# A graph layer's per-edge filters made by TensorE alone, one TensorE increment a turn, and gathers that wait for VectorE's message

## The chip, the cores and the metric

One NeuronCore of a Trainium2 chip runs the kernel. It has a matrix engine (TensorE, PE in the profile), a vector engine (VectorE, DVE), an activation engine (ScalarE, ACT), GpSimd (POOL), which here writes the descriptors of the gathers, and SyncE (SP), which starts plain transfers. The engines are ordered by semaphores: an instruction increments one when it ends, another waits until it has a value. The metric is the device time of one run in microseconds (us); lower is better.

## The reference

The kernel computes one message-passing layer on a graph with 6,250 nodes and 206,250 edges that are sorted by their target, with 128 features:

```python
h = jnp.maximum(_layernorm(x, axis=-1), 0.0)
W = silu(dist_feat @ fw1 + fb1) @ fw2 + fb2      # 206250 x 128, from 50 numbers an edge
x2 = silu(h @ aw1 + ab1) @ aw2 + ab2             # 6250 x 128, the node table
msg = W * x2[src]
agg = jax.ops.segment_sum(msg, dst, num_segments=h.shape[0])
out = silu(agg @ ow1 + ob1) @ ow2 + ob2
return x + h + out
```

## The kernel before

**Start.** The nodes lie in 49 tiles of 128, handled in 7 chunks. VectorE takes statistics (L557), ScalarE normalizes (L413), TensorE transposes and multiplies (L813, L819, L824), VectorE adds a bias (L571), and SyncE writes the rows to a node table in device memory (L321). Meanwhile GpSimd gathers 48 tiles of raw x rows (L369) for six "early" pairs; it waits ahead of some of them for a chunk of the table (`table_at`). When the whole table is written, GpSimd starts on the table gathers (L381).

**Turns.** The edges lie in 202 pairs of two groups of 4 tiles, 1,024 edges in a pair. A Python loop, `turns`, gives each engine its code for pair 0, 1, 2, ...; each engine's order is fixed when the program is written, and there is no scheduler. For pair s:

- TensorE `hidden` (L876): first filter layer into PSUM tile `hid_ps`, of which there is one. It increments `hid_sum`.
- ScalarE `silu_hid` (L444): SiLU from `hid_ps` into `hid[s % 2]`; increments `hid_done`.
- TensorE `filters` (L884): second filter layer, back into `hid_ps`, with features in the rows; increments `across`.
- ScalarE `add_fb2` (L450): adds the bias column, `hid_ps` into `hid[s % 2]`; increments `biased`.
- TensorE `by_edge` (L891): 8 transposes into `fil_ps[s % 2]`, edges in the rows; increments `fil_done`. It waits for `red_done` of pair s - 2, whose messages lay in that tile.
- VectorE `message` (L665) multiplies by the gathered rows in `xg[i % 3]` and increments `msg_done`; then a row sum (L668), a mask (L672) and a second row sum (L668), which increments `red_done`. Two one-hot tiles are built (L655, L657).
- TensorE `add_up` (L899): sums of pair s - 2 by matmuls with the one-hot tiles.

The next pair's `hidden` is issued before this pair's `by_edge`, and its `filters` after. Between the pairs stand steps of node tasks (`task`), which use a PSUM tile of their own.

**Gathers.** One pair's gathers are 8 indirect transfers of 128 rows, 8 instructions of GpSimd, into one of `XG` = 3 buffers. The early pairs have none, so that 195 pairs with 8 gathers and one with 4 make 1,564 in all. Ahead of pair s GpSimd has one wait: `pool.wait_ge(fil_done, run(s - REACH))` with `REACH` = 1. Since `by_edge` of s - 1 waited for `red_done` of s - 3, this says also that the buffer is free. `run(c)` only adds a fixed offset to a count.

## Time and profile before

| what | value |
|---|---|
| time, median of 3 runs | 2037.55 us (2035.7 to 2040.6) |
| span of the profiled execution, first to last instruction | 2356.9 us |
| time of the profiled execution outside its span | not given by the profile |
| GpSimd (POOL) busy in it | 1526.1 us, 65% |
| TensorE (PE) busy, weight loads (PEld) beside it | 1290.8 us and 700.7 us |
| VectorE (DVE), ScalarE (ACT) busy | 1191.7 us and 520.7 us |
| TensorE's granted clock, mean | 0.74 of full |

The profile is one execution, recorded by the hardware profiler. The rows below are of three kinds. A group of instructions reads: line, engine, operation, output<-inputs, shapes, count | busy us in all, mean ns of one | idle us of the engine just before them, and what ended it. A row of the timeline reads: start, us taken, engine, line, operation, and in brackets how long the engine had been idle and what ended that. "issue" is idle time for which the profile shows no waited-for instruction; "remote" is a wait whose releaser the profile could not name.

### The profile page before, as it was taken

To read this page: it belongs to the slowest core of one execution; us is meant where nothing else is said; L and a number is where in the kernel's file an instruction comes from. 1 tells how busy PE (TensorE), PEld (TensorE's weight loads), DVE (VectorE), ACT (ScalarE), POOL (GpSimd) and SP (SyncE) were. 2 spreads that over 40 slices of the span, in tenths; PEclk is the share of its full clock that TensorE was granted. 3 is DMA by queue.
4 is the path that set the end of the run, shared out by engine and by line. 5 is a ranking of instruction groups with operands and counts; after the bars stand their busy time and mean duration, and the time that the engine had idled before them with its cause. 6 is when DMAs were issued, how large, how long until landed. Compare 5 with 4: busy or idle time off the path is not lost.

```text
span 2356.9 us, 13198 instructions
## 1 busy us (share of the span) xinstructions
PE 1290.8 (55%) x4526; PEld 700.7 (30%) x4526; DVE 1191.7 (51%) x1497; ACT 520.7 (22%) x545; POOL 1526.1 (65%) x1619
## 2 busy tenths in 40 slices
PE   3454555655565557555655565555564566554645
PEld 2222333332232323223322232222232233322323
DVE  4455445555455445544544564445444454444545
ACT  3322222222121122122212221222121122121211
POOL 5556666667666666666666666666666676666665
PEclk9686777777786768776877786777686777677867
DMA  4421222212221212212212221222221222212211
GB/s 148 144 76 45 82 58 71 79 51 85 82 83 45 83 50 81 87 46 81 86 51 78 80 85 50 80 65 65 82 85 48 82 54 81 85 45 82 59 46 44
DMA packets 62293, 171.47 MB, mean 73 GB/s; under 512 B 27088, under 2 KB 29648, under 8 KB 59024
## 3 DMA queue, kind: packets, MB, share of 16 engines
q0 software_dynamic: 51584, 105.75, 16.8%
q1 hardware_dynamic: 8192, 61.32, 6.9%
q10 hardware_dynamic: 2448, 3.54, 0.4%
q8 instruction: 36, 0.59, 0.1%
q14 instruction: 33, 0.27, 0.0%
HBM read 164.08 MB, written 6.42 MB: 72 GB/s over the span
## 4 chain that ended last, share of the span: by engine, by line
another core or an unknown queue 30%; POOL 24%; PE 18%; issue 16%; ACT 9%; DVE 2%; DMA 0%; SPq 0%; POOLq 0%; ACTq 0%; DVEq 0%
POOL xg L381 24%; PE banks L884 9%; PE banks L876 4%; ACT hid L444 4%; ACT hid L450 4%; PE banks L891 2%; PE banks L824 1%; PE banks L899 1%; ACT hs L469 0%; DVE stats L557 0%; PE banks L819 0%; DMA xs<-in_x 0%; PE banks L944 0%; DVE sums L668 0%
## 5 line engine op out<-in xcount | busy, mean ns | idle before, releaser
L381 POOL DMA_INDIRECT xg<-node_table,src x1564 | 1479.0, 946 | 777.6 <-issue 451.3
L884 PE MATMUL banks<-hid,wts 128*128 128x512 f32 x806 | 534.4, 798 | 556.3 <-ACT hid L444 437.9
L665 DVE TENSOR_TENSOR banks<-banks,xg 128x1024 f32<-128x1024 f32 (+1 forms) x198 | 241.4, 1219 | 1070.2 <-DMA xg<-node_table,src 607.2
L668 DVE TENSOR_REDUCE sums<-banks 128x128 f32<-128x1024 f32 (+1 forms) x408 | 494.0, 1211 | 13.7
L876 PE MATMUL banks<-attr,wts 50*128 50x512 f32 x806 | 284.4, 786 | 383.1 <-ACT hid L450 206.4
L444 ACT ACTIVATE hid<-banks,cols 128x1024 f32<-128x1024 f32 x202 | 224.7, 1112 | 887.9 <-remote 672.4
L450 ACT ACTIVATE hid<-banks,cols 128x1024 f32<-128x1024 f32 x202 | 224.6, 1112 | 865.6 <-remote 376.6
L884 PEld LDWEIGHTS banks<-hid,wts 128*128 128x128 f32 x806 | 180.6, 249 | 746.6 <-ACT hid L444 465.7
L891 PE MATMUL banks<-ident,hid 128*128 128x128 f32 x1612 | 283.5, 333 | 40.1 <-issue 38.1
L891 PEld LDWEIGHTS banks<-ident,hid 128*128 128x128 f32 x1612 | 224.6, 170 | 237.1 <-issue 228.6
L672 DVE TENSOR_TENSOR banks<-banks,other 128x1024 f32<-128x1024 f32 (+1 forms) x204 | 248.7, 1219 | 7.0
L876 PEld LDWEIGHTS banks<-attr,wts 50*128 50x128 f32 x806 | 73.5, 220 | 446.0 <-issue 238.9
L899 PEld LDWEIGHTS banks<-onehot,sums 128*128 128x128 f32 x816 | 146.0, 227 | 126.9 <-issue 119.7
L899 PE MATMUL banks<-onehot,sums 128*128 128x88 f32 x816 | 134.1, 297 | 6.2 <-DVE sums L668 6.2
L369 POOL DMA_INDIRECT e_x<-in_x,e_src x48 | 45.8, 955 | 38.1 <-DVE res L571 22.6
L657 DVE SCALAR_TENSOR_TENSOR onehot<-iota,ends,onehot 128x88 f32<-128x88 f32 x202 | 62.5, 310 | 10.0 <-remote 2.9
L655 DVE TENSOR_SCALAR onehot<-iota,ends 128x88 f32<-128x88 f32 x202 | 55.2, 273 | 0.1
L824 PE MATMUL banks<-node_wts,mid 128*128 128x128 f32 x194 | 31.8, 323 | 21.8 <-ACT mid L420 11.6
L824 PEld LDWEIGHTS banks<-node_wts,mid 128*128 128x128 f32 x194 | 29.1, 231 | 25.6 <-ACT mid L420 23.6
L813 PE MATMUL banks<-ident,hs 128*128 128x128 f32 x97 | 16.0, 304 | 18.4 <-issue 18.4
L831 PE MATMUL banks<-wts,mid 128*128 128x128 f32 x98 | 23.9, 385 | 0.6 <-ACT mid L478 0.6
L819 PE MATMUL banks<-hT,node_wts 128*128 128x512 f32 (+2 forms) x28 | 16.2, 716 | 11.7 <-remote 11.7
(83 smaller groups left out, 282.9 us busy)
## 6 DMA issues: line engine op xcount, KB each, us to landing
attr<-in_attr SPq DMA_DIRECT2D x25, 2048.0 KB
xg<-node_table,src POOLq DMA_INDIRECT x1564
out<-res ACTq DMA_DIRECT2D x8, 256.0 KB
xs<-in_x SPq DMA_DIRECT2D x3, 512.0 KB, 6.6
node_table<-res SPq DMA_DIRECT2D x3, 512.0 KB
out<-res ACTq DMA_DIRECT2D x5, 192.0 KB
spare<-in_dst SPq DMA_DIRECT2D x1, 808.0 KB
src<-in_src SPq DMA_DIRECT2D x1, 808.0 KB
```

Source lines behind the costliest of these rows:

```text
L381: pool.indirect_dma_start(xg[:, i % XG, j, :], None, table[:, :], bass.IndirectOffsetOnAxis(ap=src[:, s * L + j:s * L + j + 1], axis=0))\
L444: act.activation(hid[:, s % 2, 0:n], hid_ps[:, 0:n], ACT.Silu, bias=cols[:, 0:1]).then_inc(hid_done, 1)
L450: act.activation(hid[:, s % 2, 0:n], hid_ps[:, 0:n], ACT.Identity, bias=cols[:, 3:4]).then_inc(biased, 1)
L657: dve.scalar_tensor_tensor(out=to[:, 1, :], in0=nodes, scalar=ends[:, 1, s:s + 1], in1=to[:, 0, :], op0=ALU.is_equal, op1=ALU.subtract).th ...
L665: dve.tensor_tensor(to, to, rows_of, ALU.mult).then_inc(signal, 1)
L668: return dve.reduce_sum(sums[:, at, m, :], of.rearrange("p j f -> p f j"), AX.X)
L672: dve.tensor_tensor(to, to, other[:, t:t + n].rearrange("p (j o) -> p j o", o=1).to_broadcast([P, n, F]), ALU.mult).then_inc(signal, 1)
L824: i = pe.matmul(to[:, j * P:(j + 1) * P], mid[:, j * P:(j + 1) * P], weights, start=True, stop=True)
L876: i = pe.matmul(hid_ps[:, GC * half:GC * half + GC], fw1_s[at, :], attr[at, cols_of], start=True, stop=True)
L884: i = pe.matmul(hid_ps[:, at], w["fw2_s"][:, :], hid[:, s % 2, at], start=True, stop=True)
L891: i = pe.transpose(fil_ps[s % 2][:, at], hid[:, s % 2, at], ident[:, :])
L899: i = pe.matmul(sum_ps[:, to:to + WIN], sums[:, at, m, :], onehot[:, s % OH_SETS, m, :], start=False, stop=stop and m == 1)
```

## The change

It has seven parts.

1. `filters` takes the SiLU output as the stationary operand, 8 matmuls of 128 columns, and so puts edges in the rows by itself. The bias comes first into the same PSUM tile, by two bf16 matmuls of 512 columns of `ones_b` with `fb2_rows`. `by_edge` and `add_fb2` are gone, and `across`, `biased` with them.
2. `hidden` runs two pairs ahead (`FILL` = 2) and follows `filters`.
3. TensorE increments one semaphore a turn, `pe_turn`, with the last matmul of `hidden(s + 2)`. Whoever waited for `hid_sum`, `fil_done`, `n_tr`, `n_l1` or `n_l2` now waits for a count of `pe_turn`.
4. VectorE's message of pair s waits for `pe_turn` at `after(s)`, which is `hidden(s + 2)`.
5. GpSimd waits, ahead of pair number i with gathers, for the message of pair number i - 3.
6. The 8 VectorE operations that split the bias into three bf16 rows (`fb2_part`, `fb2_rest`, `fb2_rows`), which ran only on a rarely used branch at the end, now stand on VectorE ahead of the first statistics, behind a wait for the `rows` transfer.
7. ScalarE's first turn applies SiLU to pairs 0 to 2, later turns to s + 2.

```diff
-REACH = XG - LAG
+FILL = 2
...
+def after(s):
+
+    return run(s + FILL)
...
-                    pool.wait_ge(fil_done, run(s - REACH))
+                    pool.wait_ge(msg_done, run(MAIN_TURNS[i - XG]))
...
             def silu_hid(s):
                 n = tiles_in(s) * P
-                act.wait_ge(hid_sum, run(s))
+                act.wait_ge(pe_turn, run(s))
                 act.activation(hid[:, s % 2, 0:n], hid_ps[:, 0:n], ACT.Silu, bias=cols[:, 0:1]).then_inc(hid_done, 1)
...
-            def add_fb2(s):
-                n = tiles_in(s) * P
-                act.wait_ge(across, run(s))
-                act.activation(hid[:, s % 2, 0:n], hid_ps[:, 0:n], ACT.Identity, bias=cols[:, 3:4]).then_inc(biased, 1)
-
             def pair(s):
-                for a in ((0, 1) if s == 0 else (s + 1,)):
+                for a in range(FILL + 1) if s == 0 else (s + FILL,):
                     if a < PAIRS:
                         silu_hid(a)
-                        add_fb2(a)
...
             dve.memset(fb2_rows[:, :, :], 0.0).then_inc(s_set, 1)
 
+            dve.wait_ge(s_rows, 16)
+            dve.wait_ge(s_set, 1)
+            dve.tensor_copy(fb2_part[:, 0, :], rows[:, 0, :]).then_inc(s_fb2, 1)
+            dve.wait_ge(s_fb2, 1)
+            dve.tensor_tensor(fb2_rest[:, 0, :], rows[:, 0, :], fb2_part[:, 0, :], ALU.subtract).then_inc(s_fb2, 1)
...
+            for i in range(3):
+                dve.tensor_copy(fb2_rows[32 * i:32 * i + 1, :, :],
+                                fb2_part[32 * i:32 * i + 1, i:i + 1, :].to_broadcast([1, TPG, F])).then_inc(s_fb2, 1)
...
-                dve.wait_ge(fil_done, run(s))
+                dve.wait_ge(pe_turn, after(s))
                 msg = by_tile(s, 0, L)
                 message(msg, rows_of, msg_done)
...
                 if s > 0:
-                    pe.wait_ge(biased, run(s - 1))
+                    pe.wait_ge(hid_done, run(s - 1))
...
             def filters(s):
+                to, halves = fil_ps[s % 2], range(tiles_in(s) // TPG)
+                pe.wait_ge(red_done, run(s, LAG))
+                for h in halves:
+                    pe.matmul(to[:, GC * h:GC * h + GC], ones_b[:, :], fb2_rows.rearrange("p j f -> p (j f)"), start=True, stop=False)
                 pe.wait_ge(hid_done, run(s))
-                for h in range(tiles_in(s) // TPG):
-                    at = slice(GC * h, GC * h + GC)
-                    i = pe.matmul(hid_ps[:, at], w["fw2_s"][:, :], hid[:, s % 2, at], start=True, stop=True)
-                i.then_inc(across, 1)
...
                 for j in range(tiles_in(s)):
                     at = slice(j * P, (j + 1) * P)
-                    i = pe.transpose(fil_ps[s % 2][:, at], hid[:, s % 2, at], ident[:, :])
-                i.then_inc(fil_done, 1)
+                    i = pe.matmul(to[:, at], hid[:, s % 2, at], w["fw2_s"][:, :], start=False, stop=j % TPG == TPG - 1)
+                return i
...
             def pair(s):
                 if s == 0:
-                    hidden(s)
-                    filters(s)
-                if s + 1 < PAIRS:
-                    hidden(s + 1)
+                    for a in range(FILL):
+                        hidden(a)
+                i = filters(s)
+                if s + FILL < PAIRS:
+                    hidden(s + FILL)
                 else:
-                    pe.wait_ge(biased, run(s))
-                pe.wait_ge(red_done, run(s, LAG))
-                by_edge(s)
-                if s + 1 < PAIRS:
-                    filters(s + 1)
+                    i.then_inc(pe_turn, 1)
                 for a in SUMS_AT.get(s, ()):
                     pair_sums(a)
```

TensorE in a turn in the middle of the loop. Before, with `banks0` for `hid_ps`, `banks1` and `banks2` for the two tiles of `fil_ps`, and `banks3` for the sums:

```order
L876 MATMUL banks0<-attr,wts 128x512 [waits biased]
L876 MATMUL banks0<-attr,wts 128x512
L891 MATMUL banks1<-ident,hid 128x128 [waits red_done]
L891 MATMUL banks1<-ident,hid 128x128 x7
L884 MATMUL banks0<-hid,wts 128x512 [waits hid_done]
L884 MATMUL banks0<-hid,wts 128x512
L899 MATMUL banks3<-onehot,sums 128x88 x2
```

The same engine and place with the change:

```order
L894 MATMUL banks1<-fb2_rows,ones_b 128x512 [waits red_done]
L894 MATMUL banks1<-fb2_rows,ones_b 128x512
L898 MATMUL banks1<-wts,hid 128x128 [waits hid_done]
L898 MATMUL banks1<-wts,hid 128x128 x7
L886 MATMUL banks0<-attr,wts 128x512 [waits hid_done]
L886 MATMUL banks0<-attr,wts 128x512
L906 MATMUL banks3<-onehot,sums 128x88 x2
```

The 8 transposes of 128 columns and 2 matmuls of 512 have become 8 matmuls of 128 and 2 bf16 matmuls of 512, and `banks0` is written once a turn and not twice.

VectorE from its first instructions to the second operation on the moments, before:

```order
L548 MEMSET ones 128x128
L549 MEMSET ones_b 128x128
L550 MEMSET none_b 128x256
L551 MEMSET fb_rows 128x256
L557 BN_STATS stats<-xs 128x6 x24
L519 TENSOR_TENSOR moments<-stats 128x24
L520 TENSOR_TENSOR moments<-stats 128x24
```

With the change:

```order
L559 MEMSET fb_rows 128x256
L563 CAST fb_part<-rows 128x128
L565 TENSOR_TENSOR fb_rest<-rows,fb_part 128x128
L567 CAST fb_part<-fb_rest 128x128
L569 TENSOR_TENSOR fb_rest<-fb_rest,fb_part 128x128
L571 CAST fb_part<-fb_rest 128x128
L574 COPY fb_rows<-fb_part 1x512 x3
L581 BN_STATS stats<-xs 128x6 x24
```

Eight operations have come between the memsets and the statistics. GpSimd's instructions stay in their order; of its table gathers only the semaphore changes that the first of each 8 waits for.

## Rows read from the trace of the kernel before

**Rows 1.** The page: span, then each engine's busy time, share and instructions.
```profile
span 2356.9 us, 13198 instructions
PE 1290.8 (55%) x4526; PEld 700.7 (30%) x4526; DVE 1191.7 (51%) x1497; ACT 520.7 (22%) x545; POOL 1526.1 (65%) x1619
```

**Rows 2.** Groups of GpSimd's instructions.
```profile
L381 POOL DMA_INDIRECT xg<-node_table,src x1564 | 1479.0, 946 | 777.6 <-issue 451.3 <-remote 277.4 <-PE banks L891 39.1
L369 POOL DMA_INDIRECT e_x<-in_x,e_src x48 | 45.8, 955 | 38.1 <-DVE res L571 22.6 <-issue 13.7 <-DMA e_src<-in_e_src 1.8
```

**Rows 3.** Timeline of GpSimd: its last three gathers.
```profile
2339.13 0.94 POOL L381 DMA_INDIRECT xg<-node_table,src  x1 [0.30 <-issue]
2340.38 0.95 POOL L381 DMA_INDIRECT xg<-node_table,src  x1 [0.31 <-issue]
2341.63 0.95 POOL L381 DMA_INDIRECT xg<-node_table,src  x1 [0.30 <-issue]
```

**Rows 4.** Timeline of GpSimd from the start: the gathers that it waited for.
```profile
3.76 1.10 POOL L369 DMA_INDIRECT e_x<-in_x,e_src  x1 [1.80 <-DMA e_src<-in_e_src]
...
45.98 0.95 POOL L369 DMA_INDIRECT e_x<-in_x,e_src  x1 [12.37 <-DVE res L571]
...
76.04 0.95 POOL L369 DMA_INDIRECT e_x<-in_x,e_src  x1 [10.20 <-DVE res L571]
...
95.66 0.94 POOL L381 DMA_INDIRECT xg<-node_table,src  x1 [9.77 <-DMA node_table<-res]
```

**Rows 5.** Timeline of all engines around 960 us, late releases.
```profile
958.15 2.08 PE L876 MATMUL banks<-attr,wts 50*128 50x512 f32 x4 [13.77 <-issue]
958.89 0.95 POOL L381 DMA_INDIRECT xg<-node_table,src  x1 [0.30 <-issue]
...
960.16 1.97 PE L891 MATMUL banks<-ident,hid 128*128 128x128 f32 x8
964.03 1.11 ACT L444 ACTIVATE hid<-banks,cols 128x1024 f32<-128x1024 f32 x1 [5.93 <-remote]
964.19 1.23 DVE L665 TENSOR_TENSOR banks<-banks,xg 128x1024 f32<-128x1024 f32 x1 [5.90 <-remote]
964.36 0.95 POOL L381 DMA_INDIRECT xg<-node_table,src  x1 [4.52 <-remote]
```

**Rows 6.** Timeline of all engines from 139 us, prompt releases and full clock.
```profile
139.47 1.13 PE L876 MATMUL banks<-attr,wts 50*128 50x512 f32 x4 [1.21 <-ACT hid L450]
...
140.53 1.10 PE L891 MATMUL banks<-ident,hid 128*128 128x128 f32 x8
140.65 1.11 ACT L444 ACTIVATE hid<-banks,cols 128x1024 f32<-128x1024 f32 x1 [1.23 <-PE banks L876]
...
141.81 1.98 PE L884 MATMUL banks<-hid,wts 128*128 128x512 f32 x4 [0.19 <-issue]
...
143.63 0.37 PE L909 MATMUL banks<-none_b,ones_b 128*128 128x491 bf16 x1
```

**Rows 7.** Timeline of TensorE: the same operations elsewhere, at either clock.
```profile
40.67 3.78 PE L824 MATMUL banks<-node_wts,mid 128*128 128x128 f32 x16 [4.26 <-ACT mid L420]
...
47.87 2.05 PE L824 MATMUL banks<-node_wts,mid 128*128 128x128 f32 x16 [0.33 <-ACT mid L420]
...
1005.35 3.78 PE L884 MATMUL banks<-hid,wts 128*128 128x512 f32 x4 [5.42 <-ACT hid L444]
1008.93 0.99 PE L899 MATMUL banks<-onehot,sums 128*128 128x88 f32 x4
```

**Rows 8.** The instructions of the one bf16 matmul line: ns min/median/max.
```profile
L909 PE MATMUL banks<-none_b,ones_b x15: 280/371/619, 143.6 to 2309.2; 128*128 128x491 bf16 x13, 128*128 128x460 bf16 x1, 128*128 128x274 bf16 x1
```

**Rows 9.** Groups of instructions from 120 to 2330 us: VectorE's operations of a turn.
```profile
L668 DVE TENSOR_REDUCE sums<-banks 128x128 f32<-128x1024 f32 x399 | 488.3, 1224 | 13.4
L672 DVE TENSOR_TENSOR banks<-banks,other 128x1024 f32<-128x1024 f32 x199 | 245.2, 1232 | 6.8
L665 DVE TENSOR_TENSOR banks<-banks,xg 128x1024 f32<-128x1024 f32 x193 | 237.9, 1233 | 1053.7 <-DMA xg<-node_table,src 606.9 <-remote 433.4 <-PE banks L891 7.5
```

**Rows 10.** Timeline of VectorE and ScalarE's queue in the first 20 us.
```profile
1.20 0.45 ACTq L397 DMA_DIRECT2D rows<-in_rows  x1
...
2.18 0.27 DVE L551 MEMSET fb_rows<- 128x256 uint32 x1
...
12.79 0.20 DVE L519 TENSOR_TENSOR moments<-stats 128x24 f32<-128x24 f32 x1
13.02 0.20 DVE L520 TENSOR_TENSOR moments<-stats 128x24 f32<-128x24 f32 x1
```

**Rows 11.** The transfers: KB each, and us from issue to landing.
```profile
rows<-in_rows ACTq DMA_DIRECT2D x1, 192.0 KB, 6.4
```

**Rows 12.** The instructions of two lines of VectorE and what it waited for ahead of the first.
```profile
L557 DVE BATCH_NORM_STATS2 stats<-xs x49: 274/276/296, 7.8 to 21.5; 128x6 f32<-128x128 f32 x49
  DMA xs<-in_x: 5.3, 1
  issue: 1.7, 3
...
L735 DVE COPY hT<-banks x12: 679/680/682, 255.1 to 1346.9; 128x512 f32<-128x512 f32 x12
```

More of the change, by code:

```diff
@@ L150, in table_writes, with turn_of @@
     return sum(len(transfers(i)) for i in range(c + 1))
+def turn_of(kind, n, step):
+    return TASKS[TASK_OF[kind, n]][2] + (EARLY_STEPS if kind == "early" else OUT_STEPS)[step]
 def turns(pair, task):
@@ L287, in gnn_layer @@
         e_gathered = [sem(f"e_gathered{r}") for r in range(EARLY_PAIRS)]
[L288 to L289 removed]
+        pe_turn, hid_done, oh_done, msg_done, masked, first_done, red_done, half_msg, half_first, half_masked, half_red, win_done, group_done = (
+            sem(n) for n in ("pe_turn", "hid_done", "oh_done", "msg_done", "masked", "first_done", "red_done", "half_msg",
                              "half_first", "half_masked", "half_red", "win_done", "group_done"))
[L291 to L292 removed]
+        n_relu, n_hT, n_mid, n_rows, last_l1, last_l2 = (
+            sem(n) for n in ("n_relu", "n_hT", "n_mid", "n_rows", "last_l1", "last_l2"))
         r_din, r_key, r_in, r_gat, r_l1, r_hid, r_fil, r_msg, r_one, r_win, r_add, r_taken = (
@@ L328, in pair @@
                     if s >= 2 * PART:
-                        sp.wait_ge(hid_sum, run(s - PART - 1))
+                        sp.wait_ge(pe_turn, run(s - PART - 1))
                     at = s % (2 * PART) * GC
@@ L398, in _ @@
             act.dma_start(cols[:, :], cols_t).then_inc(s_cols, 16)
-            for ahead in (s_h, s_mid, a_mid, hid_done, biased):
+            for ahead in (s_h, s_mid, a_mid, hid_done):
                 act.sem_inc(ahead, AHEAD)
@@ L463, in task @@
                     if n >= 2:
-                        act.wait_ge(n_tr, n - 1)
+                        act.wait_ge(pe_turn, after(turn_of("early", n - 2, "copied")))
                     if n == 0:
@@ L473, in task @@
                     width, bias = (GC, 1) if kind == "early" else (OUTS[n][1] * P, 2)
-                    act.wait_ge(n_l1, b + 1)
-                    if b > 0:
-                        act.wait_ge(n_l2, b)
-                    source = last_ps_1 if kind == "out" and n == len(OUTS) - 1 else node_ps
+                    last = kind == "out" and n == len(OUTS) - 1
+                    if last:
+                        act.wait_ge(last_l1, 1)
+                    else:
+                        act.wait_ge(pe_turn, after(turn_of(kind, n, "middle")))
+                    source = last_ps_1 if last else node_ps
                     act.activation(mid[:, 0:width], source[:, 0:width], ACT.Silu, bias=cols[:, bias:bias + 1])\
@@ L716, in by_halves @@
                 i, k, n = MAIN_OF[s], HALVED.index(s), tiles_in(s) // 2
-                dve.wait_ge(fil_done, run(s))
+                dve.wait_ge(pe_turn, after(s))
                 for h in range(2):
@@ L733, in task @@
                 if step == "copied":
-                    dve.wait_ge(n_tr, n + 1)
+                    dve.wait_ge(pe_turn, after(turn_of(kind, n, "copied")))
                     dve.tensor_copy(hT[:, 0:GC], node_ps).then_inc(n_hT, 1)
                 elif step == "rows" and kind == "early":
-                    dve.wait_ge(n_l2, b + 1)
+                    dve.wait_ge(pe_turn, after(turn_of(kind, n, "rows")))
                     dve.tensor_tensor(e_x[:, n * TPG:(n + 1) * TPG, :], node_ps.rearrange("p (j f) -> p j f", f=F),
@@ L747, in task @@
                     if to is yc:
-                        dve.wait_ge(n_l2, b + 1)
+                        dve.wait_ge(pe_turn, after(turn_of(kind, n, "rows")))
                     dve.tensor_tensor(to, to, rows[:, 2:3, :].to_broadcast([P, tiles, F]), ALU.add).then_inc(s_xs, 1)
                     if to is xc:
-                        dve.wait_ge(n_l2, b + 1)
+                        dve.wait_ge(last_l2, 1)
                     if n >= 2:
@@ L810, in _, with transposes @@
         def _(pe):
[L811 removed]
+            def transposes(to, b, n_tiles):
                 for j in range(n_tiles):
                     i = pe.transpose(to[:, j * P:(j + 1) * P], hs[:, b, j, :], ident[:, :])
[L814 removed]
+                return i
             def layer1(source, n_tiles, weights, summed):
@@ L836, in node_transposes @@
                 pe.wait_ge(s_hT, run(c, 1))
-                transposes(tr_ps, b, TILES[c], s_tr)
+                transposes(tr_ps, b, TILES[c]).then_inc(s_tr, 1)
             def node_layer1(c):
@@ L846, in node_layer2 @@
                 pe.wait_ge(s_res, run(c, 1))
-                layer2(l2_ps, TILES[c], w["aw2_s"][:, :], s_l2)
-            for ahead in (s_tr, s_l1, s_l2, a_l1, a_l2, hid_sum, across, fil_done):
+                layer2(l2_ps, TILES[c], w["aw2_s"][:, :]).then_inc(s_l2, 1)
+            for ahead in (s_tr, s_l1, s_l2, a_l1, a_l2, pe_turn):
                 pe.sem_inc(ahead, AHEAD)
@@ L932, in task @@
                         pe.wait_ge(n_rows, b)
-                    transposes(node_ps, n % 2, TPG, n_tr)
+                    transposes(node_ps, n % 2, TPG)
                 elif step == "first" and kind == "early":
                     pe.wait_ge(n_hT, n + 1)
-                    pe.matmul(node_ps, w["aw1_s"][:, :], hT[:, 0:GC], start=True, stop=True).then_inc(n_l1, 1)
+                    pe.matmul(node_ps, w["aw1_s"][:, :], hT[:, 0:GC], start=True, stop=True)
                 elif step == "first":
@@ L943, in task @@
                     nodes = slice(LEAD + first * P, LEAD + (first + tiles) * P)
-                    pe.matmul((last_ps_1 if last else node_ps)[:, 0:tiles * P], w["ow1_s"][:, :], agg[:, nodes], start=True, stop=True).then_inc(n_l1, 1)
+                    i = pe.matmul((last_ps_1 if last else node_ps)[:, 0:tiles * P], w["ow1_s"][:, :], agg[:, nodes], start=True, stop=True)
+                    if last:
+                        i.then_inc(last_l1, 1)
                 elif step == "second":
```

50 lines of the change are left out of this document (19 added, 31 removed).

## The prediction

> **What bounds the kernel now.** I read the page first, then GpSimd's groups, then the timeline. No engine is busy for more than 65% of the span, and the busiest is GpSimd [rows 1]. Its 1,564 table gathers take 946 ns each, and each is followed by about 0.30 us of "issue" when nothing holds it up [rows 2, 3], so that gathers start 1.25 us apart: 2339.13, 2340.38, 2341.63. A pair of 8 costs GpSimd 10.0 us. VectorE's four large operations of a pair cost 1.23 + 1.22 + 1.23 + 1.22 = 4.9 us [rows 9]. TensorE's turn is, at full clock, 1.13 + 1.10 + 1.98 [rows 6] and about 0.5 for the sums (half of the 0.99 at the lower clock [rows 7]), 4.7 us; at the lower clock 2.08 + 1.97 [rows 5] + 3.78 + 0.99 [rows 7] = 8.8 us. Each is under 10.0. If nothing waited, GpSimd alone would set the time: first gather at 3.76 [rows 4], 48 + 1,564 = 1,612 gathers at 1.25 us = 2015.0, and from the last start, 2341.63, to the end of the span 15.3 [rows 1, 3]. That is 2034.1 us.
>
> The profiled execution is 2356.9 us long, and the runs have a median of 2037.55, which is 319.4 less. The difference has its place: in the trace the table gathers waited 277.4 for "remote" and 39.1 for the transposes of TensorE, 316.5 in all [rows 2]. Without them the span would be 2040.4, within 3 us of the median.
>
> What GpSimd waits for there is an increment that comes late. Around 960 us the first layer ends at 958.15 + 2.08 = 960.23 and the transposes at 962.13, but ScalarE starts at 964.03, VectorE at 964.19 and GpSimd at 964.36: 3.8 and 2.1 us late, and all three together [rows 5]. At 139 us the same first layer ends at 140.60 and ScalarE starts at 140.65 [rows 6]. VectorE's four operations of a turn, which wait for one another by semaphores too, have 13.4 + 6.8 us of idle time ahead of some 600 instructions [rows 9]: they are not held up. So TensorE's increments are late in the profiled execution, by microseconds, in many turns.
>
> The question is whether they are late in an execution that is not recorded. If GpSimd's 1.25 us holds there too, the median leaves 2037.55 - 2034.1 = 3.4 us for every wait together, and part of that is the wait for the node table at the start. I take this as the likelier case: two numbers that have nothing to do with each other, 316.5 and 319.4, agree. The Trainium skill, page "NOTIFIC — the notification-queue block", section "7.1 Overflow: three behaviours, one of which stalls the engine", says that the block which writes the profiler's records holds back an engine rather than lose a record inside it; that would make the lateness a thing of the recording. The trace doesn't show that block; it is in keeping with the 319.4. The page "Runtime: NRT & Kernel Launch", section "The ~15µs preamble/postamble breakdown", has the profile only about 6.2 us above the reported time, by which the span would be 2043.8; the rows here disagree, by 313 us.
>
> **The change, part by part**, for a run without late increments.
>
> *TensorE's turn.* It loses 8 transposes, 1.10 at full clock and 1.97 at the lower one, and the old second layer, 1.98 and 3.78. It gains 8 matmuls with `hid` stationary; the nearest rows are L824's 8 of that shape: 2.05 and 3.78 [rows 7]. It gains two bf16 matmuls of 512 columns, each at most 0.37 and 0.62 [rows 8]. A turn becomes 1.13 + 2.05 + 0.74 + 0.5 = 4.4 us, or 2.08 + 3.78 + 1.24 + 0.99 = 8.1 us: 0.3 to 0.7 less than before. Either way it lies beside GpSimd's 10.0, so it is worth 0. The cover that is left at the lower clock is 1.9 us.
>
> *ScalarE* loses an operation of 1.1 us a turn. It was busy 22% of the span [rows 1]: worth 0.
>
> *VectorE's message waits for `hidden(s + 2)`.* At the lower clock TensorE needs 1.24 + 3.78 + 2.08 = 7.1 us from `red_done` of s - 2 to that increment. `red_done` of s - 2 comes 4.9 us after its rows, and rows of s come 20.0 after those of s - 2. That leaves 20.0 - 4.9 - 7.1 = 8.0 us: 0.
>
> *GpSimd's wait.* When it has issued pair s - 1, the message of s - 3 is long done: its rows came about 20 us before, less the transfer's time. Before, the wait was for transposes that could start when VectorE was done with s - 3, 4.9 + 1.97 = 6.9 us after its rows. Both are over by then: 0. Of the trace's 316.5 us the new wait would save much, since it asks only for what VectorE has already done.
>
> *Eight VectorE operations at the start.* The `rows` transfer is issued at 1.20 and lands 6.4 later, at 7.6 [rows 10, 11]; the statistics start at 7.8 [rows 12], so the wait is hidden. Five chained operations of 128 columns go at the 0.23 us of 12.79 to 13.02: 1.15. Three copies of 512 columns are not in the trace: at least 0.20 each (the short operations [rows 10]), at most 0.68 (a copy of 512 f32 [rows 12]); I take the memset of the same bytes, 0.27 [rows 10], since these are bf16. The sum is 1.15 + 0.8 = 2.0, bounds 1.8 and 3.2. VectorE was idle 1.7 us between later statistics [rows 12], so between 0 and 3.2 reaches the table. GpSimd waited for the table or its chunks three times, 12.37, 10.20 and 9.77 [rows 4], so I count all of 2.0.
>
> *The first turns* may give back up to the same, when the fourth pair's gathers no longer wait for TensorE's third turn. I take 0.5.
>
> Sum: 2.0 - 0.5 = +1.5 us, and 2037.55 + 1.5 = 2039.0. Against the profiled execution's own time the same sum would be 2358.4, if its 316.5 us of waits stayed; I expect them to shrink by about half, to a span near 2200, and count on none of it.
>
> **The rivals.**
>
> *The increments are late in every execution.* Then GpSimd must be quicker than 1.25 us when it isn't recorded: each 0.01 us a gather makes 16 us of room (1,612 gathers), so at 1.22 us there would be 3.4 + 48 = 52 us of waits. For it: each gather carries a record too, and the waits recur all through the trace. Against it: the agreement of 316.5 and 319.4. The change would take some two thirds, as two of three increments a turn are gone and GpSimd's wait doesn't need TensorE: 2037.55 - 35 = about 2003. It decides from 4 us of waits on, a pace under 1.25 by 0.01 us.
>
> *The start takes longer* (slower). If the `rows` transfer lands later than 7.6, beside the load of x, or the three copies cost 0.68, the chain from statistics to node table moves by 3.2 plus the lateness, and GpSimd's whole stream with it. It decides from 4.1 us on, 0.2% of the time, so it needs a landing about 1 us late. With 2 us late it gives 2037.55 + 5.2 = 2042.8. For it: GpSimd waits for that chain three times [rows 4]. Against it: 1.7 us of slack inside [rows 12].
>
> *TensorE at the lower clock becomes the bound.* A turn of 8.1 us plus a node task's four matmuls of L824's shape, half of 3.78, is 10.0, level with GpSimd, but only in some turns. Its price: up to 1 us in 25 turns. I count it in with the second rival.
>
> **How the numbers follow.** 0.2% of the median is 4.1 us, about what a measurement of this kernel can tell from no change; the three runs span 4.9. No change 0.53, late increments 0.32, slower start or turns 0.15. The predicted time is that of the likeliest, 2039.0, its own range 2035 to 2042. The range reaches down past 2003 to 1988 (waits of 75 us, two thirds gone) and up to 2045 (3.2 + 4 us late); some 2 in 10 lie outside.
>
> **What would show it.** If I am right, the times agree while the profile changes much: GpSimd's waits far under 316.5, the second layer's 8 matmuls near 2.05 or 3.78 us, no waits of VectorE of more than a turn, and the pace still 1.25 us. A first table gather later than 95.66 by some 2 us, apart from late increments, shows the start. If the time falls by over 4 us, the step "the lateness belongs to the recording" is wrong; if it rises by more, the start or a wait of VectorE for `pe_turn` is.

## The result

| kernel | median | runs | ratio, 95% |
|---|---|---|---|
| before | 2039.68 us | 2035.7 to 2040.6, 6 runs | 1 |
| with the change | 2032.73 us | 2030.81 to 2032.97, 6 runs | 0.9968 (0.9957 to 0.998) |

The change makes the kernel faster by 7 us, 0.32%. The forecast was no change, 2039.0, and the time lies outside its own range of 2035 to 2042.

One fact is needed to read every number below: the time of these kernels differs from chip to chip. The experiments ran on five chips. On chips 3, 6 and 7 the kernel before takes 2037.3, 2036.9 and 2037.3 us, on chips 1 and 4 it takes 2346.3 and 2358.0. Within a chip all executions are of one kind. Each chip was used in one stretch of time only, so the record can't tell the chip from the hour. I call the first kind prompt chips and the second kind late chips. The profile of before came from an execution of the late kind (span 2356.9), which is none of the six in the table; the median of 2037.55 beside it is of the prompt kind, and so are both medians of the table. Ratios are always to the kernel before on the same chip.

The page of the changed kernel, an execution of the prompt kind; against it stand [rows 1]:

```profile
span 2028.9 us, 15293 instructions
PE 1214.7 (60%) x5635; PEld 915.1 (45%) x5735; DVE 1194.5 (59%) x1505; ACT 297.2 (15%) x343; POOL 1522.7 (75%) x1619
```

Its groups of GpSimd (before: [rows 2]) and its chain of work that ended last:

```profile
L393 POOL DMA_INDIRECT xg<-node_table,src x1564 | 1475.9, 944 | 477.5 <-issue 476.3 <-DMA node_table<-res 1.2
L381 POOL DMA_INDIRECT e_x<-in_x,e_src x48 | 45.6, 951 | 16.1 <-issue 14.3 <-DMA e_src<-in_e_src 1.8
...
POOL 72%; issue 24%; DMA 1%; DVE 1%; PE 1%; ACT 0%; POOLq 0%; SPq 0%; ACTq 0%; DVEq 0%
```

Where before, in its late execution, had 277.4 us of "remote" and 39.1 of TensorE, nothing but "issue" is left and one wait of 1.2 us for the table. The timeline of GpSimd, first gather, first table gather (before: [rows 4]) and the last two gathers (before: [rows 3]):

```profile
3.77 1.10 POOL L381 DMA_INDIRECT e_x<-in_x,e_src  x1 [1.81 <-DMA e_src<-in_e_src]
...
64.88 0.94 POOL L393 DMA_INDIRECT xg<-node_table,src  x1 [1.16 <-DMA node_table<-res]
...
2014.93 0.94 POOL L393 DMA_INDIRECT xg<-node_table,src  x1 [0.30 <-issue]
2016.17 0.94 POOL L393 DMA_INDIRECT xg<-node_table,src  x1 [0.30 <-issue]
```

The last gather starts at 2016.17, 12.7 us before the end of the span. From the first table gather there are 1,563 steps in 1951.3 us, 1.248 us each: the kernel is now GpSimd's unbroken row of gathers, a start and an end. The time of this execution is 2030.81, its span 2028.9, so 1.9 us lie outside the span. Of the matmuls of L894 (the bias) the profile has records for 303 out of 403. What the other engines wait for, and the two new matmul lines (ns min/median/max):

```profile
ACT hid L456 <- PE banks L886: 1630.1, 202, 12.6
DVE banks L688 <- DMA xg<-node_table,src: 751.0, 182, 5.8
...
PE banks L894 <- DVE sums L691: 671.9, 173, 6.9
```
```profile
L898 PE MATMUL banks<-wts,hid x3224: 272/421/426, 81.0 to 2010.8; 128*128 128x128 f32 x190
...
L894 PE MATMUL banks<-fb_rows,ones_b x303: 379/610/634, 80.5 to 1999.2; 128*128 128x512 bf16 x152
```

The three engines wait for gathered rows or for one another, and none of them makes GpSimd wait.

### The profile page after: what moved, and what is told of

Its sections match the earlier page's. It is cut to its first block, busy times and chain, and to the rows that moved or that the text cites. A ratio compares the mean times of both kernels' runs of the same rounds, so it can differ in the third digit from the quotient of the medians.

```text
span 2028.9 us, 15293 instructions
## 1 busy us (share of the span) xinstructions
PE 1214.7 (60%) x5635; PEld 915.1 (45%) x5735; DVE 1194.5 (59%) x1505; ACT 297.2 (15%) x343; POOL 1522.7 (75%) x1619
## 4 chain that ended last, share of the span: by engine, by line
POOL 72%; issue 24%; DMA 1%; DVE 1%; PE 1%; ACT 0%; POOLq 0%; SPq 0%; ACTq 0%; DVEq 0%
POOL xg L393 72%; DMA node_table<-res 1%; DVE res L595 0%; DMA rows<-in_rows 0%; DVE stats L581 0%; PE banks L828 0%; DVE sums L691 0%; PE banks L822 0%; ACT hs L425 0%; DMA xg<-node_table,src 0%; DVE hT L547 0%; PE banks L833 0%; DVE xs L553 0%; DVE banks L695 0%; DVE banks L688 0%
## 5 line engine op out<-in xcount | busy, mean ns | idle before, releaser
L898 PEld LDWEIGHTS banks<-wts,hid 128*128 128x128 f32 x3224 | 633.8, 291 | 60.0 <-issue 37.9
L898 PE MATMUL banks<-wts,hid 128*128 128x128 f32 x3224 | 622.4, 375 | 3.5 <-DVE sums L691 3.5
L894 PE MATMUL banks<-fb_rows,ones_b 128*128 128x512 bf16 x303 | 149.2, 558 | 674.3 <-DVE sums L691 671.9
L456 ACT ACTIVATE hid<-banks,cols 128x1024 f32<-128x1024 f32 x202 | 224.5, 1111 | 1630.1 <-PE banks L886 1630.1
L894 PEld LDWEIGHTS banks<-fb_rows,ones_b 128*128 128x128 bf16 x403 | 28.9, 110 | 710.4 <-DVE sums L691 688.3
L886 PE MATMUL banks<-attr,wts 50*128 50x512 f32 x806 | 261.6, 729 | 1.5 <-ACT hid L456 1.3
L906 PEld LDWEIGHTS banks<-onehot,sums 128*128 128x128 f32 x816 | 109.0, 194 | 148.5 <-issue 142.2
L940 PE MATMUL banks<-hT,node_wts 128*128 128x512 f32 x24 | 23.2, 1066 | 51.9 <-DVE hT L758 51.9
L948 PE MATMUL banks<-agg,wts 128*128 128x512 f32 (+2 forms) x28 | 17.7, 721 | 20.0 <-DVE e_x L762 14.9
L833 PEld LDWEIGHTS banks<-node_wts,mid 128*128 128x128 f32 x194 | 23.1, 192 | 9.8 <-issue 5.5
```

The source lines that it names most:

```text
L456: act.activation(hid[:, s % 2, 0:n], hid_ps[:, 0:n], ACT.Silu, bias=cols[:, 0:1]).then_inc(hid_done, 1)
L833: i = pe.matmul(to[:, j * P:(j + 1) * P], mid[:, j * P:(j + 1) * P], weights, start=True, stop=True)
L886: i = pe.matmul(hid_ps[:, GC * half:GC * half + GC], fw1_s[at, :], attr[at, cols_of], start=True, stop=True)
L894: pe.matmul(to[:, GC * h:GC * h + GC], ones_b[:, :], fb2_rows.rearrange("p j f -> p (j f)"), start=True, stop=False)
L898: i = pe.matmul(to[:, at], hid[:, s % 2, at], w["fw2_s"][:, :], start=False, stop=j % TPG == TPG - 1)
L906: i = pe.matmul(sum_ps[:, to:to + WIN], sums[:, at, m, :], onehot[:, s % OH_SETS, m, :], start=False, stop=stop and m == 1)
```

## Experiments on late chips: is the lateness the recording's?

**The kernel before, unchanged (chip 1).**

> The kernel before once more, unchanged. It gives a second profiled execution. If TensorE's late increments were an accident of the one execution recorded first, the span is near 2036 us (2 us under the time, as the changed kernel's 2028.9 stands to 2030.8) and GpSimd's waits on table gathers are a few us. If they come whenever this kernel is recorded, the span is again near 2350 with some 300 us of waits. Time: ratio 1.000 within 0.002 by either.

Measured: 2345.72 us (ratio 0.9995, 0.9973 to 1.0017), profile span 2351.2. GpSimd's waits:

```profile
POOL xg L381 <- issue: 454.7, 1478, 1.7
POOL xg L381 <- remote: 246.7, 72, 5.4
POOL xg L381 <- PE banks L891: 63.8, 13, 11.8
```

246.7 + 63.8 us against 277.4 + 39.1 in [rows 2]: an execution of the same kind. All ten executions of this kernel here take 2340.8 to 2353.1. They, and all others of the experiments, have a span and a granted clock on record, those on prompt chips too. So recording alone doesn't make the lateness. Whether a late chip would be late without any recording, no run shows.

The next three expectations were written for a prompt chip. What they asked is answered in the next section; here the same kernels show what the late kind does.

**GpSimd's wait alone (chip 1).** The kernel before with one line changed:

```diff
-                    pool.wait_ge(fil_done, run(s - REACH))
+                    pool.wait_ge(msg_done, run(MAIN_TURNS[i - XG]))
```

> The kernel before with one line changed: GpSimd waits for VectorE's message three gathered pairs back, as in the change. Theory one (the gain is GpSimd's wait in the first turns, where TensorE and ScalarE need more than 8 us a turn at the lower clock and start late): 2039.7 falls by 7 to 9 us, to 2031 to 2033, since it has the gain without the 2.5 us that the eight VectorE operations cost the start. Theory two (the gain needs the shorter TensorE and ScalarE chain, because messages themselves come late in the first turns): under 3 us faster.

Measured: 2425.04 us, ratio 1.0291 (1.0243 to 1.0339). GpSimd's waits, and the timeline of one stop:

```profile
POOL xg L381 <- issue: 472.3, 1497, 2.2
POOL xg L381 <- DVE banks L665: 359.8, 66, 15.2
```
```profile
1017.82 2.08 PE L876 MATMUL banks<-attr,wts 50*128 50x512 f32 x4 [6.80 <-issue]
...
1019.83 1.97 PE L891 MATMUL banks<-ident,hid 128*128 128x128 f32 x8
...
1023.10 0.95 POOL L381 DMA_INDIRECT xg<-node_table,src  x1 [0.30 <-issue]
1027.81 1.11 ACT L444 ACTIVATE hid<-banks,cols 128x1024 f32<-128x1024 f32 x1 [10.12 <-remote]
1027.97 1.23 DVE L665 TENSOR_TENSOR banks<-banks,xg 128x1024 f32<-128x1024 f32 x1 [9.80 <-remote]
...
1029.47 0.95 POOL L381 DMA_INDIRECT xg<-node_table,src  x1 [5.42 <-DVE banks L665]
```

TensorE was done with both at 1019.90 and 1021.80. ScalarE and VectorE learn of it at 1027.81 and 1027.97, 7.9 and 6.2 us later, and 3.8 us after GpSimd's last gather ended (1024.05). So GpSimd asks for a message that started only after GpSimd itself had stopped, and the message's own 1.23 us come on top of each stop. In the two timelines the stops (starts of neighbouring gathers more than 1.95 us apart) are 79 in the run above, each 3.61 us over the ordinary 1.25 on average, and 74 here, each 4.76 over it: 1.15 more a stop. Between the first and the last table gather that is 67 of the 73 us by which the span is longer.

**The changed kernel with the eight operations behind the statistics (chip 1).** The block of seven waits and eight operations moves from ahead of `bn_stats` to behind the last table bias.

> The changed kernel with the eight VectorE operations that split the bias moved from ahead of the first statistics to behind the last chunk of the node table. Theory one (they stand on the path to the table, 7.78 to 10.01 in the profile of after): the first table gather starts about 2 us earlier than 64.88, at 63.7 at the least, since GpSimd is busy with the raw rows until then, and the time falls by 1.2 us, to 2031.5. Theory two (they were hidden): no change within 0.5 us.

Measured: 2406.15 us, ratio 1.024 (1.0202 to 1.0277), waits for the message 349.1 us in 63.

**The changed kernel with TensorE's wait (chip 1).**

```diff
-                    pool.wait_ge(msg_done, run(MAIN_TURNS[i - XG]))
+                    pool.wait_ge(pe_turn, after(s - 1))
```

> The changed kernel with GpSimd waiting, as before, for TensorE to be done with the filters of the pair ahead, here at the count of the one increment a turn. Theory one (the gain is GpSimd's wait alone, whatever TensorE's order): it returns to 2039 to 2041 us. Theory two (the new TensorE order with one increment is itself fast enough that the old wait costs nothing): 2032.7, the same as the changed kernel within 1 us.

Measured: 2346.65 us, ratio 0.9997 (0.9976 to 1.0018), waits 269.1 us in 69 and 35.6 in 8. One increment a turn where there were three, and a turn of TensorE without `by_edge` and `add_fb2`, change nothing on a late chip. The message's wait costs 60 to 79 us on the late chips.

**The changed kernel and a fourth buffer (chip 4).** `XG = 4` in the changed kernel, beside it unchanged.

> The changed kernel unchanged. With prompt increments 2031 (ratio 0.9965), as in two comparisons so far. On a chip with late increments it has not run; the kernel with the eight operations behind the statistics took 2406 there, so 2405 (ratio 1.024), slower than the kernel before.

> The changed kernel with four buffers of gathered rows in place of three, GpSimd's wait then being for the message of four pairs before. With prompt increments nothing is left to save, as GpSimd waits for nothing: 2031, the same as the changed kernel. On a chip with late increments GpSimd could issue 32 gathers and not 24 before it stops, so the stops are fewer: 42 in place of 60, at 5.5 us each about 100 us less, near 2310 (ratio 0.985); if the increments stay away until GpSimd stops, whatever the number of buffers, each stop costs the same and their number alone counts.

Measured: changed kernel 2430.0 us, ratio 1.0294 (1.0242 to 1.0345), waits 371.0 us in 67; with four buffers 2437.16, ratio 1.0329 (1.0281 to 1.0376):

```profile
POOL xg L393 <- issue: 471.2, 1497, 2.7
POOL xg L393 <- DVE banks L688: 363.6, 66, 12.0
```

There are 72 stops with three buffers and 75 with four, and 24 gathers (three pairs) lie between most of them in both, 56 and 53 times. My expectation of 42 stops and 2310 us was wrong: the number of stops isn't set by the buffers. What sets it, I can't show. In the kernel before 16 gathers between two stops are as common as 24 (39 and 31 times in the trace of [rows 2]).

## Experiments on prompt chips: where do the 7 us come from?

**The changed kernel, and the kernel before with four buffers (chip 3).** The latter's edit is `XG = 4`, by which `REACH` becomes 2.

> The changed kernel, unchanged, beside the kernel before on one chip. What the last four runs showed: where TensorE's increments come late (the kernel before takes 2346 us), GpSimd issues 24 gathers and then waits 4 us, and the wait for the message adds the 1.23 us of the message to each wait. Theory one (the wait for the message costs): where the kernel before takes about 2346, this takes 2400 to 2425, 2.4 to 3.3% slower. Theory two (the eight operations moved later were what cost in the run that had them moved): 2346. Where increments are prompt (the kernel before takes about 2040), this takes 2033 by both.

> The kernel before with four buffers for gathered rows in place of three, so that GpSimd may issue 32 gathers before it waits for TensorE. Theory one (a burst ends in one wait of about 4 us, whatever its length, in which the late increments come in): where increments are late, the 65 bursts become 49 and some 65 to 80 us go, to about 2275. Theory two (increments are late by a time that has nothing to do with the burst): GpSimd has 10 us more of slack a turn and most of the 280 us go, to about 2080. Theory three (the longer GpSimd runs, the later they come): no gain. Where increments are prompt: 2039, or 2036 where the first turns' wait goes.

Measured: 2030.51 us, ratio 0.9962 (0.9949 to 0.9976), and 2030.57, ratio 0.9963 (0.995 to 0.9976). With four buffers GpSimd waits 1.2 us for TensorE in all, in 4 times of the ordinary 0.30. The expectation had 2039, or 2036, for a prompt chip and was 5 us too high. So the gain is waits of GpSimd for `fil_done` in the kernel before, and a fourth buffer takes them away as well.

**The kernel before, for its profile (chip 6).**

> The kernel before unchanged, for a profile of it on a chip where its increments come promptly (its time then is near 2037, not 2346). Theory A (GpSimd waits for TensorE's filter turns in the first pairs and in some node turns): the trace shows 5 to 8 us of waits of the edge gathers on TensorE's filter line, nearly all ahead of 140 us and at the node tasks, and a span near 2035.5. Rival B (the gain lies in the tail behind the last gather): no such waits, the last gather at 2016 to 2018 and a tail of 15 us or more. If the increments are late on this chip, 2346 and stalls of 4 us after each 24 gathers as before.

Measured: 2036.72 us, ratio 0.9997 (0.9987 to 1.0007), span 2034.4. GpSimd's waits, and the timeline of the longest one:

```profile
POOL xg L381 <- issue: 474.8, 1558, 0.3
...
POOL xg L381 <- PE banks L891: 7.9, 6, 3.7
```
```profile
951.10 1.22 DVE L668 TENSOR_REDUCE sums<-banks 128x128 f32<-128x1024 f32 x1
...
952.25 0.68 DVE L739 TENSOR_TENSOR e_x<-banks,rows 128x512 f32<-128x512 f32 x1
...
953.07 2.04 PE L944 MATMUL banks<-agg,wts 128*128 128x512 f32 x2 [5.10 <-DVE e_x L739]
...
954.62 0.95 POOL L381 DMA_INDIRECT xg<-node_table,src  x1 [0.30 <-issue]
...
955.05 2.08 PE L876 MATMUL banks<-attr,wts 50*128 50x512 f32 x4
957.06 1.97 PE L891 MATMUL banks<-ident,hid 128*128 128x128 f32 x8
...
959.30 0.94 POOL L381 DMA_INDIRECT xg<-node_table,src  x1 [3.73 <-PE banks L891]
```

Read it from below. GpSimd stands until 959.30 for the transposes (L891), which end at 959.03. They come behind `hidden` (L876) and behind the first matmul of an output task (L944), which had waited 5.1 us for VectorE's `rows` step of the early task before it (L739). That step stands behind VectorE's whole pair. Only two of the six waits are long, 3.7 us here and 2.7 at 556 us, where the same chain L739, L944, L876, L891 stands with L944 at 551.04. There the transposes took 1.09, as at full clock, so the chain doesn't need the lower clock at its end. Together the two are 5.8 us over the ordinary 0.30 a gather; the span of the changed kernel, from another chip, is 2034.4 - 2028.9 = 5.5 shorter. Theory A was right on the size and on the node turns, and wrong in putting nearly all of it ahead of 140 us: there stands one wait of 0.50, at 94.45. Rival B fails: the 12.7 us behind the last gather are the same in both kernels.

**Does this chain cause it (chips 4 and 7)?** The kernel before with its own wait; the task list alone differs:

```diff
-        if outs and ready(outs[0]) <= s:
+        if outs and ready(outs[0]) <= s and not (done and done[-1][0] == "early" and s == free):
```

> The kernel before, with its old wait of GpSimd and its old order of TensorE; only the list of node tasks differs: an output task no longer begins in the turn behind the last step of an early task (it begins one turn later), so TensorE's first matmul of it doesn't wait for VectorE's rows. Theory A (the 6 us of GpSimd's waits of the kernel before all come from TensorE standing behind that matmul, at 553 and 953 us, in turns at the lower clock): the two waits of 2.7 and 3.7 us go, and the time is that of the changed kernel, ratio 0.997 of before. Rival B (any turn at the lower clock with a node task is too long for the old wait, wherever the task's list puts it): the waits come back in other turns and the ratio stays 1.000. On a chip with late increments: 2346, ratio 1.000 by both.

> The kernel before with the list of node tasks alone changed, as in the run before, for a chip with prompt increments. Theory A (the waits of the kernel before come from the two turns in which TensorE stands behind the first matmul of an output task): ratio 0.997, no wait of GpSimd for the transposes above 0.5 us. Rival B (any turn with a node task at the lower clock is too long for the old wait): ratio 1.000, waits in other turns. With late increments 1.000 by both.

Measured on chip 4 (late): 2364.37, ratio 1.0018 (0.9992 to 1.0043). On chip 7: 2030.79, ratio 0.9971 (0.9961 to 0.9982). The waits there:

```profile
POOL xg L381 <- issue: 475.4, 1560, 0.3
...
POOL xg L381 <- PE banks L891: 1.7, 4, 0.8
```

L944 no longer waits for `rows` (five times, 18.8 us in all, in the kernel before), and the whole gain is there without the change. Theory A holds: the 6 us were these two turns. In the changed kernel the delay of TensorE is still there, and only GpSimd no longer stands behind it:

```profile
551.25 2.04 PE L948 MATMUL banks<-agg,wts 128*128 128x512 f32 x2 [5.30 <-DVE e_x L762]
```

**Which part of the change takes the waits away (chip 6)?** The two edits of chip 1 again, and the moved operations:

> The kernel before with the message's wait alone. On a chip with prompt increments: if TensorE's order is the cause of the gain, the time stays at 2037 or rises a little, for VectorE's message comes behind the same late filter turn (ratio 1.000 to 1.002). If the message itself is the cause, 2031 (ratio 0.9965). On a chip with late increments 2425, as before.

> The changed kernel, but GpSimd waits for TensorE's one increment of the turn in place of the message of VectorE. On a chip with prompt increments: if the new order of TensorE is what takes GpSimd's waits away, the time is that of the changed kernel, 2031 (ratio 0.9965). If the message, which frees the rows without TensorE's increment, is what does it, 2037 (ratio 1.000). On a chip with late increments 2346.

> The changed kernel with the eight VectorE operations behind the statistics. On a chip with prompt increments: if they delay the first table gather by what they take (1.6 to 2.0 us), the time is 2029 (ratio 0.9955) and the first table gather starts at 63.5; if GpSimd is busy with the gathers of raw rows until 63.7 anyway, 2031 or 1 us less at most. On a chip with late increments 2406, as before.

| kernel | median | ratio, 95% | GpSimd's waits for another engine in the turns |
|---|---|---|---|
| before, message's wait | 2030.55 us | 0.9967 (0.9955 to 0.9979) | none |
| changed, TensorE's wait | 2047.03 us | 1.0048 (1.0034 to 1.0062) | 23.0 us in 17 |
| changed, operations later | 2030.20 us | 0.9965 (0.9951 to 0.9978) | none |

The message's wait alone is the whole gain. It is the diff's one line for GpSimd; the new order of TensorE without it loses 10 us, which neither of my expectations held. Its waits:

```profile
POOL xg L393 <- issue: 471.7, 1547, 0.5
POOL xg L393 <- PE banks L886: 23.0, 17, 5.0
```
```profile
554.38 0.94 POOL L393 DMA_INDIRECT xg<-node_table,src  x1 [0.30 <-issue]
560.36 0.94 POOL L393 DMA_INDIRECT xg<-node_table,src  x1 [5.04 <-PE banks L886]
```

Nine of the 17 waits are above 0.4 us. Two are the turns of before, now 5.0 and 4.9 us in place of 2.7 and 3.7; the other seven, 0.5 to 2.3 us, stand in turns in which the kernel before doesn't wait.

The operations' place: the first table gather starts at 64.20 with them later and at 64.88 with them at the start.

**Why does TensorE's wait lose more in the new order (chips 4 and 7)?** The kernel above, with an increment of its own behind the second layer:

```diff
-                    pool.wait_ge(pe_turn, after(s - 1))
+                    if s - 1 + FILL < PAIRS:
+                        pool.wait_ge(fil_end, run(s - 1))
+                    else:
+                        pool.wait_ge(pe_turn, after(s - 1))
...
                 if s + FILL < PAIRS:
+                    i.then_inc(fil_end, 1)
                     hidden(s + FILL)
```

> The changed kernel with GpSimd waiting for TensorE as before, but for an increment of its own at the end of the second layer, and not for the one behind the first layer of s + 2. Theory A (the 10 us that the kernel with one increment and TensorE's wait lost, 2047 against 2037, come from the place of the increment, 2 us later at the lower clock, in some ten turns): the time lies at 2031 to 2038, ratio 0.997 to 1.001. Rival B (TensorE's new turn itself is later at those turns, since the second layer waits for VectorE's sums and then takes 3.8 us where the transposes took 2.0): at least 2042, ratio 1.003 or more. On a chip with late increments 2346.

> The changed kernel with GpSimd waiting for an increment at the end of TensorE's second layer, for a chip with prompt increments. Theory A (the 10 us that the wait for the one increment of a turn lost come from its place): 2031 to 2038, ratio 0.997 to 1.001. Rival B (the new turn itself is later): 2042 or more, ratio 1.003 or more. With late increments 0.997 as measured.

Measured on chip 7: 2039.87, ratio 1.0013 (1.0004 to 1.0022), waits 12.7 us in 12. On chip 4 (late): 2354.07, ratio 0.9971 (0.9948 to 0.9995). So about 7 of the 10 us lost are the place of the increment (1.0048 against 1.0013). The time lies between theory A's range, up to 2038, and rival B's, from 2042: neither held as put, and A has the larger part. About 2.6 us are left. They are in keeping with rival B's ground, which no run tests: behind VectorE's sums now stand the 8 matmuls of L898, 3.47 us in one such turn, where the transposes took 1.97.

**What the landing of gathers does (chips 3 and 7).** The kernel before, with GpSimd waiting for the landing of the last pair's gathers ahead of every third pair:

```diff
+                if i >= XG and i % 3 == 0 and s not in HALVED:
+                    pool.wait_ge(gathered[(i - 1) % XG], ((i - 1) // XG + 1) * 16 * L)
```

> The kernel before with one wait added: ahead of every third pair GpSimd waits until the gathers of the pair ahead have landed. Theory one (late increments come in as soon as no gather is in flight): where increments are late, each of the 65 bursts ends in a wait of 1.6 us for landing and TensorE's increments are then there, so that 4.2 becomes 1.6 and the time falls by 170 us, to about 2180. Theory two (they need a longer quiet of GpSimd, as the 3.8 us after its last gather ended suggest): the added wait changes nothing there, 2346 within 15, since GpSimd waits for TensorE right after it. Where increments are prompt, the wait costs 65 times 1.6, 105 us: 2144.

> The kernel before with GpSimd waiting, ahead of every third pair, for the landing of the last pair's gathers. With prompt increments 2184 (ratio 1.071), as measured: 65 waits of 2.5 us. With late increments: if they come through as soon as GpSimd has stopped and its gathers have landed, this wait takes the place of the stops of 3.8 us and the time is near 2184 plus a few waits, 2190 to 2230 (ratio 0.93 to 0.95); if they come for another reason, both waits add up, 2450 or more.

Measured: 2184.31 us, ratio 1.0714 (1.0697 to 1.073), and 2183.59, ratio 1.0718 (1.0702 to 1.0735). The waits for the landing are 152.2 us in 60, about 2.5 each (the first expectation had 1.6 each, and 2144 for the time), so on a prompt chip the stops cost about what they last, 147 us. Whether the landing releases late increments, no run shows: both chips were prompt.

## Why the prediction was wrong

**The floor and the room above it.** The prediction found GpSimd at its pace of 1.25 us to be the bound of the median: right, and the changed kernel runs at 1.248 without a break. But the floor of 2034.1 was too high by 6.4 us. It took 15.3 us behind the start of the last gather from the late profile, where a prompt chip shows 12.7. It took 1.25 us where a prompt chip shows 1.248, which is 2.6 us over all gathers. And it counted 1,612 gathers up to the start of the last one, where there are 1,611 steps. It was also a span, set against a time that is 1.9 us longer than its span. That hid room: of the median's 2037.55 only 3.4 us seemed left for all waits, and the prompt profile of before has 7.9 us of them on one line alone, 6.1 over the usual 0.30 each.

**"Both are over by then: 0".** This is the step of the sum that failed. The sum's term for GpSimd's new wait should have been -5.8 us. I compared one ordinary turn: transposes 6.9 us after the rows of s - 3, message long done. I left out that `by_edge` of s - 1 also stands behind all that TensorE has queued ahead of it, and in the turn after an early task that is a matmul waiting for VectorE's last step of that task. The ordinary turn was right; two turns out of 202 were not. The third rival named node tasks at the lower clock, but as length of work (8.1 + 1.9), in the changed kernel and as a loss of up to 1 us; it was a wait inside the kernel before.

**"The lateness belongs to the recording".** Wrong as put: a recorded execution of the same kernel on chip 6 has a span of 2034.4, and on chip 1 all executions are late, 2346 in the median. That 316.5 us of waits agreed with 319.4 between span and median was in part luck. Against the prompt profile the late one is 322.5 us longer: 31.4 ahead of the first table gather (95.66 against 64.30), 288.6 between the first and the last, 2.5 behind. The 316.5 leave out the start, and they hold the ordinary 0.30 us of 90 gathers, 27 us. The prediction had put a fall of over 4 us down to this step; the fall came from the one above. The wrong kind of profile did its harm there: it hid the two turns among some 90 waits. The Trainium skill, page "NOTIFIC — the notification-queue block", section "7.1 Overflow: three behaviours, one of which stalls the engine", says that the block holds back an engine rather than lose a record inside it. That this made the profile long was my own step, and no run here shows it. The Trainium skill, page "Runtime: NRT & Kernel Launch", section "The ~15µs preamble/postamble breakdown", has the profile's total about 6.2 us above the reported time. Here the span is 1.7 to 2.0 us below the time in every execution that lists both.

**Late increments in every execution.** The rival had 2003 and "GpSimd's wait doesn't need TensorE", two thirds of the waits gone. On chips that are late the change costs 2.9% instead. The message does need TensorE: VectorE's message of s - 3 waits for `pe_turn`, which TensorE increments. With it goes "of the trace's 316.5 us the new wait would save much": 371.0 us are waited for, not less. The forecast span near 2200 belongs to no run.

**TensorE's turn: 0 for the time, as said.** At the lower clock L898 takes 0.42 us, so that 8 take 3.4 and not 3.78, and L894 takes 0.61, at most 0.63, against a bound of 0.62 that I had from 491 columns. The new order is worth 0 where GpSimd waits for the message, and costs 10 us where GpSimd waits for TensorE: the cover of 1.9 us that I named wasn't enough in nine turns. ScalarE: 0, as said (busy 15%). VectorE's own wait for `pe_turn`, 0 in the prediction, is 26.2 us in 5 times in the changed kernel, all hidden: GpSimd doesn't wait.

**Eight VectorE operations: +2.0 in the sum, 0.7 measured.** They take what was said and a little more:

```profile
7.53 0.23 DVE L563 CAST fb_part<-rows 128x128 bf16<-128x128 f32 x1 [5.08 <-DMA rows<-in_rows]
...
8.96 1.01 DVE L574 COPY fb_rows<-fb_part 1x512 bf16<-1x512 bf16 x3
10.01 2.22 DVE L581 BATCH_NORM_STATS2 stats<-xs 128x6 f32<-128x128 f32 x11
```

From 7.53 to 10.01 are 2.5 us, the three copies 1.01 and not 0.8, and the transfer landed at 7.5 as forecast. Statistics start 2.2 us later than in [rows 12]. But the table gathers start only 0.7 later. The three waits of [rows 4] from which I passed all of it on, 12.37, 10.20 and 9.77, are of a late chip. On a prompt one GpSimd is busy with the 48 raw gathers until 63.7 (62.78 + 0.94 in the changed kernel); the table is ready by then in the kernel before and 1.2 us later in the changed one.

**The first turns.** -0.5 in the sum; the fourth pair's wait in the prompt profile of before is 0.50 against the usual 0.30, so -0.2.

With the terms as measured: -5.8 - 0.2 + 0.7 = -5.3 us, against -5.5 in the spans, -6.8 between the medians on chip 3 and -7 between the first ones. The 1.5 us beyond the terms lie within what executions of the kernel before differ by (2036.5 to 2041.3 on chip 3) and have no cause on record.

## What to carry to other kernels

When an in-order engine signals "free" at the end of a long queue, don't judge the wait by the ordinary turn: list what each engine has queued ahead of the increment in the rarest kind of turn. Wait for the event that frees the resource and not for a later one that implies it, but count who must act for that event: where it hangs on a third engine, its delay is added. If a profile's span and the timed median differ by 15%, get a profile of the timed kind before any step of the argument rests on a wait.

## What the hardware showed

I had not expected the same kernel to take 2037 us on three chips and 2346 to 2358 on two. On the late ones, while GpSimd issues gathers without a pause, TensorE's increments reach other engines up to 8 us after the matmul's end in the rows shown. In [rows 5] they come to ScalarE, VectorE and GpSimd within 0.33 us of one another. After the end of GpSimd's last gather it took 3.8 us in the stop of chip 1, and 3.0 to 4.3 in the medians of six late profiles, until ScalarE or VectorE next started. VectorE's increment is not late there: its message ends at 1029.20 and GpSimd starts at 1029.47. TensorE too stands idle between single matmuls at times, with nothing that the profile shows to wait for: 455.5 us in 386 times ahead of L898 in the changed kernel on chip 4, and none on a prompt chip. From that profile:

```profile
1022.72 0.37 PE L898 MATMUL banks<-wts,hid 128*128 128x128 f32 x1 [1.73 <-issue]
...
1026.22 0.37 PE L898 MATMUL banks<-wts,hid 128*128 128x128 f32 x1 [1.73 <-issue]
...
1041.47 1.95 PE L898 MATMUL banks<-wts,hid 128*128 128x128 f32 x16
```

Single instructions of the second layer stand 1.7 us apart, and less than 20 us later all 16 of a turn (two for each of its 8 matmuls) take 1.95. What makes a chip late, what spaces the stops, and whether the late increments and TensorE's gaps are one effect or two, stays open.
